# Layer 3's first batch projected inside layer 2's last batch, and projections led by four steps

## The reference, cut to what matters

```python
# layer 2: masked attention with 8 heads of 16
scores = einsum('bhnd,bhmd->bhnm', q, k) / sqrt(D)
w = softmax(where(mask, -inf, scores), axis=-1)
out = einsum('bhnm,bhmd->bhnd', w, v)          # then @ Wo.T + bo
# layer 3: graph attention with 8 heads of 16
Wh = (h @ W).reshape(b, n, H, HD).transpose(0, 2, 1, 3)
e = e1[:, :, :, None] + e2[:, :, None, :]      # e1 = Wh @ a1, e2 = Wh @ a2
e = where(mask, -inf, e); e = where(e >= 0, e, 0.2 * e)
h_prime = einsum('bhij,bhjd->bhid', softmax(e, axis=-1), Wh)
```

## Time and profile before

| | us |
|---|---|
| runs | 745.53, 745.69, 747.58 (median 745.69) |
| profiled execution, time | 745.24 |
| its span, first to last instruction | 743.5 |
| TensorE busy | 663.1 (89%) |
| VectorE busy | 604.3 (81%) |
| ScalarE busy | 541.3 (73%) |
| GpSimd busy | 493.5 (66%) |
| mean granted TensorE clock | 0.972 |

### The profile page before, as it was taken

One profiled execution on the slowest core, in us unless ns is written; L12 is line 12 of the kernel. 1 busy time (PEld: TensorE's weight loads), 2 busy tenths in 40 slices (PEclk: granted clock), 3 DMA queues, 4 the chain that ended last, 5 costly groups with the idle time before them and its releaser, 6 DMA issues.

```text
span 743.5 us, 17518 instructions
## 1 busy us (share of the span) xinstructions
PE 663.1 (89%) x6402; PEld 495.5 (67%) x6402; DVE 604.3 (81%) x1534; ACT 541.3 (73%) x855; POOL 493.5 (66%) x522
## 2 busy tenths in 40 slices
PE   2999699999679999999999996899999999999973
PEld 1788577777446766666666666677777777777752
DVE  3599859999677888888888884888888888888882
ACT  1555389988468777777777773598888888888882
POOL 6377529999765466656667654466766677777685
PEclk9999999999789999999999998999999999999996
DMA  8900000000000000000000000000000000000001
GB/s 233 282 4 1 1 1 1 2 1 2 0 1 2 1 2 3 1 2 1 2 2 2 2 2 0 2 2 2 29 17 16 15 16 16 17 28 16 16 16 42
DMA packets 28885, 14.91 MB, mean 20 GB/s; under 512 B 1920, under 2 KB 28800, under 8 KB 28800
## 3 DMA queue, kind: packets, MB, share of 16 engines
q1 hardware_dynamic: 25344, 12.59, 6.1%
q10 hardware_dynamic: 3456, 1.20, 0.8%
HBM read 9.59 MB, written 4.19 MB: 19 GB/s over the span
## 4 chain that ended last, share of the span: by engine, by line
PE 59%; DVE 12%; issue 11%; POOL 9%; ACT 5%; POOLq 4%; DVEq 0%; ACTq 0%
PE pair L1009 20%; POOL X L528 5%; PE pair L1140 5%; PE quad L1107 4%; POOLq L523 4%; PE pair L1201 4%; DVE arena L987 2%; DVE nmx L993 2%; PE quad L1057 2%; PE pair L1112 2%; PE pair L1126 2%; PE pair L1118 2%; PE pair L1076 2%; PE quad L1047 2%; PE quad L1068 2%
## 5 line engine op out<-in xcount | busy, mean ns | idle before, releaser
L630 POOL TENSOR_TENSOR arena<-arena,nmx 128x1024 f32<-128x1024 f32 x64 | 121.3, 1895 | 90.5 <-DVE nmx L933 88.9
L644 POOL TENSOR_TENSOR arena<-arena,nmx 128x1024 f32<-128x1024 f32 x64 | 121.3, 1896 | 82.7 <-DVE nmx L993 82.7
L1009 PE MATMUL pair<-identf,arena 128*128 128x128 f32 x1088 | 152.0, 282 | 0.5 <-ACT arena L831 0.5
L1009 PEld LDWEIGHTS pair<-identf,arena 128*128 128x128 f32 x1088 | 117.9, 142 | 31.0 <-issue 30.3
L528 POOL TENSOR_SCALAR X<-yb,ln 128x128 f32<-128x128 f32 x256 | 113.5, 455 | 9.0 <-issue 9.0
L522 POOL TENSOR_TENSOR ln<-ln,neghalf 128x4 f32<-128x4 f32 x64 | 66.6, 1041 | 37.9 <-DVE ln L562 37.8
L818 ACT ACTIVATE arena<-quad 128x1024 f32<-128x1024 f32 x64 | 66.1, 1033 | 31.5 <-PE quad L1191 31.5
L926 DVE TENSOR_TENSOR arena<-quad,mask 128x1024 f32<-128x1024 f32 x64 | 77.7, 1215 | 4.8 <-PE quad L1107 4.1
L933 DVE TENSOR_REDUCE nmx<-arena 128x8 f32<-128x1024 f32 x64 | 78.0, 1218 | 1.7
L993 DVE TENSOR_REDUCE nmx<-arena 128x8 f32<-128x1024 f32 x64 | 78.0, 1218 | 1.7
L987 DVE TENSOR_TENSOR arena<-quad,arena 128x1024 f32<-128x1024 f32 x64 | 77.7, 1214 | 0.0
(11 more groups left out here) (203 smaller groups left out, 1438.4 us busy)
## 6 DMA issues: line engine op xcount, KB each, us to landing
X<-in_x SPq DMA_DIRECT2D x16, 256.0 KB, 5.8
arena<-in_adj SPq DMA_DIRECT2D x16, 256.0 KB, 6.3
out<-X SPq DMA_DIRECT2D x16, 256.0 KB, 2.3
nat_all<-in_L_gnn_W ACTq DMA_DIRECT2D x2, 64.0 KB, 4.8
w<-in_L_gnn_W ACTq DMA_DIRECT2D x2, 64.0 KB, 5.5
nat_all<-in_L_gnn_W_loop ACTq DMA_DIRECT2D x1, 64.0 KB, 2.6
nat_all<-in_L_gnn_Wg_loop ACTq DMA_DIRECT2D x1, 64.0 KB, 3.2
hg_bias<-in_L_gnn_b_loop ACTq DMA_DIRECT2D x1, 64.0 KB, 5.1
```

The source lines that it names most:

```text
L630: nc.gpsimd.tensor_tensor(v3(P2[t % 3], HEADS), v3(P2[t % 3], HEADS), nmx2[t % 2][:].unsqueeze(2).broadcast_to([128, HEADS, N]), ALU.add)\
L644: nc.gpsimd.tensor_tensor(v3(p, HEADS), v3(p, HEADS), nmx2[(t - 1) % 2][:].unsqueeze(2).broadcast_to([128, HEADS, N]), ALU.add)\
L1009: last = nc.tensor.transpose(dst[:, cols(i)], src[:, cols(i)], identf[:])
```

## The change

Layer 3's step t now goes with layer 2's step 64 + t, five steps sooner. The first batch of layer 3 is prepared within layer 2's steps 60 to 64 (new branches of `layer2`: X transposes in bank 6, the other three pieces in bank 7). Scores of graphs 0 to 5 are issued at the head of `layer2`'s step in TensorE's list (`LAP = 6`). `AHEAD` is 4 in place of 5, so from batch 1 on every piece comes one step later against the scores (X transposes at j=0, logit terms j=1, terms' transposes j=2, values j=3; the split at j=2), and ScalarE's copy of the values now stands behind its pT copy, ahead of the scaling, one step later. Layer 3's buffers in turn are shifted (`rows_of`, `y_of`, `out_bank`, `pv_bank`), with waits for layer 2's last readers. New functions `scores`, `logit_terms`, `terms_back`, `values` and `split_e` hold the same instructions as before; removed lines that only moved into them are cut, and so are the renamings of `P2[...]` to `rows_of(...)` on GpSimd and ScalarE.

```diff
@@ -46 @@
-AHEAD, BEHIND = 5, 13
+AHEAD, BEHIND = 4, 13
+LAP = 6
@@ -82 @@
         layer2(t)
-    for t in range(-AHEAD, GRAPHS + BEHIND):
-        layer2(GRAPHS + AHEAD + t)
+    for t in range(GRAPHS + BEHIND):
+        layer2(GRAPHS + t)
         layer3(t)
@@ -222 @@
         def y_of(L, b):
-            return yb[b % 4 if L == 3 else b % 2]
+            return yb[(b + 2) % 4 if L == 3 else b % 2]
@@ -233 @@
-        def early(t):
-            return bank[3] if t < 0 else bank[6]
+        def rows_of(t):
+            return P2[(t + GRAPHS) % 3]
+        def pv_bank(g):
+            return bank[6] if g < GRAPHS - 1 else bank[4]
...
         def out_bank(b):
-            return bank[6] if b < BATCHES - 2 else bank[4]
+            return bank[5] if b == BATCHES - 2 else bank[6]
@@ -537 @@
             if L == 3:
-                if b < 2:
-                    dve.wait_ge(sem("L2_norm_done"), BATCHES - 1 + b)
+                if b in (2, 3):
+                    dve.wait_ge(sem("L2_norm_done"), BATCHES - 3 + b)
                 need(dve, sem("L3_norm_done"), b - 3)
@@ -762 @@
                     nc.scalar.copy(xT[(b + 1) % 2][:], proj(t - 1)).then_inc(sem("L2_xT"), 1)
+                if t in (GRAPHS - 3, GRAPHS + 1):
+                    first = t - GRAPHS + 3 >> 2
+                    act.wait_ge(sem("L3_xT_mm"), first + 1)
+                    nc.scalar.copy(xT[first][:], bank[6]).then_inc(sem("L3_xT"), 1)
+                if t == GRAPHS - 1:
+                    act.wait_ge(sem("L3_eT_mm"), 1)
+                    nc.scalar.copy(eT[0][:], bank[7].bitcast(BF16)[:, 0:W]).then_inc(sem("L3_eT"), 1)
+                if t == GRAPHS:
+                    act.wait_ge(sem("L3_v_mm"), 1)
+                    act.wait_ge(sem("L2_pv_mm"), GRAPHS - G)
+                    nc.scalar.copy(vx[0][:].rearrange("p (a c) -> p a c", c=HP)[:, :, 0:HD],
+                                   v3(bank[7], G * HEADS)).then_inc(sem("L3_v"), 1)
                 if j == 1 and real(b):
@@ -786 @@
                     need(act, sem("L2_out_mm"), t - 4)
-                    nc.scalar.copy(oT[(t - 3) % 2][:], bank[6][:, 0:2 * N]).then_inc(sem("L2_oT"), 1)
+                    nc.scalar.copy(oT[(t - 3) % 2][:], pv_bank(t - 3)[:, 0:2 * N]).then_inc(sem("L2_oT"), 1)
                 if graph(t - 1):
@@ -803 @@
                 b, k = (t + AHEAD - 1) // G, (t + AHEAD - 1) % G
-                if real(b):
-                    if k == 0:
+                if real(b) and b > 0:
+                    if k == 0 and b > 1:
                         act.wait_ge(sem("L3_xT_mm"), b + 1)
                         need(act, sem("L3_v_mm"), b - 1)
-                        nc.scalar.copy(xT[b % 2][:], early(t - 1)).then_inc(sem("L3_xT"), 1)
+                        nc.scalar.copy(xT[b % 2][:], bank[6]).then_inc(sem("L3_xT"), 1)
                     if k == 2:
...
                         need(act, sem("L3_s_mm"), G * (b - 1))
-                        nc.scalar.copy(eT[b % 2][:], early(t - 1).bitcast(BF16)[:, 0:W]).then_inc(sem("L3_eT"), 1)
+                        nc.scalar.copy(eT[b % 2][:], bank[6].bitcast(BF16)[:, 0:W]).then_inc(sem("L3_eT"), 1)
+                    if k == 3:
+                        act.wait_ge(sem("L3_v_mm"), b + 1)
+                        need(act, sem("L3_pv_mm"), G * (b - 1))
+                        nc.scalar.copy(vx[b % 2][:].rearrange("p (a c) -> p a c", c=HP)[:, :, 0:HD],
+                                       v3(bank[6], G * HEADS)).then_inc(sem("L3_v"), 1)
                 if graph(t):
@@ -820 @@
                     nc.scalar.copy(oT[g % 2][:], bank[7][:, 0:2 * N]).then_inc(sem("L3_oT"), 1)
-                if k == 3 and real(b):
-                    act.wait_ge(sem("L3_v_mm"), b + 1)
-                    need(act, sem("L3_pv_mm"), G * (b - 1))
-                    nc.scalar.copy(vx[b % 2][:].rearrange("p (a c) -> p a c", c=HP)[:, :, 0:HD],
-                                   v3(early(t - 1), G * HEADS)).then_inc(sem("L3_v"), 1)
...
+        def split_e(dve, b, o):
+            e = v3(o[:, 0:G * 2 * HEADS], G)
+            dve.wait_ge(sem("L3_e_mm"), b + 1)
+            need(dve, sem("L3_eT_mm"), b)
+            for part in range(3):
+                at = v3(ep[:], G)[:, :, 32 * part:32 * part + 2 * HEADS]
+                need(dve, sem("L3_split"), 5 * b + 2 * part)
+                nc.vector.tensor_copy(at, e).then_inc(sem("L3_split"), 1)
+                if part < 2:
+                    dve.wait_ge(sem("L3_split"), 5 * b + 2 * part + 1)
+                    nc.vector.tensor_tensor(e, e, at, ALU.subtract).then_inc(sem("L3_split"), 1)
@@ -925 @@
                       .then_inc(sem("L2_masked"), 1)
+                if t == GRAPHS - 2:
+                    split_e(dve, 0, bank[7])
                 if j == 2 and real(b - 3):
@@ -968 @@
                 b, k = (t + AHEAD - 1) // G, (t + AHEAD - 1) % G
-                if k == 1 and real(b):
...
+                if k == 1 and real(b) and b > 0:
+                    split_e(dve, b, bank[6])
                 b, j = t // G, t % G
                 if graph(t - 1):
-                    p = P2[(t - 1) % 3]
+                    p = rows_of(t - 1)
+                    if t <= 3:
+                        dve.wait_ge(sem("L2_pT_mm"), GRAPHS - 3 + t)
+                    if t <= 2:
+                        dve.wait_ge(sem("L2_less_max"), GRAPHS - 2 + t)
                     dve.wait_ge(sem("L3_scaled"), t)
@@ -1076 @@
+            def scores(t):
+                b, j = t // G, t % G
+                if not graph(t):
+                    return
+                if j == 0:
+                    pe.wait_ge(sem("L3_eT"), b + 1)
+                if t < 2:
+                    pe.wait_ge(sem("L2_masked"), GRAPHS)
+                need(pe, sem("L3_leaky"), t - 1)
+                for i in range(2):
+                    o = bank[2 * (t % 2) + i]
+                    mm(o, identb[:], heads_of(mask2, b, j), start=True, stop=False)
+                    mm(o, eT[b % 2][:, cols(j)], sel1[:, cols(i, HQ * 128)], start=False, stop=False)
+                    for h in range(HQ):
+                        last = mm(o[:, cols(h)], sel2[:, cols(HQ * i + h)], eT[b % 2][:, cols(j)],
+                                  start=False, stop=h == HQ - 1)
+                last.then_inc(sem("L3_s_mm"), 1)
+            def logit_terms(b, o):
+                for i in range(G):
+                    last = mm(o[:, cols(i, 2 * HEADS)], xT[b % 2][:, cols(i)], wh_w[:, D:], start=True, stop=True)
+                last.then_inc(sem("L3_e_mm"), 1)
+            def terms_back(b, o):
+                pe.wait_ge(sem("L3_split"), 5 * (b + 1))
+                for i in range(G):
+                    last = nc.tensor.transpose(o.bitcast(BF16)[:, cols(i)], ep[:, cols(i)], identb[:])
+                last.then_inc(sem("L3_eT_mm"), 1)
+            def values(b, o):
+                for i in range(G):
+                    last = mm(o[:, cols(i)], xT[b % 2][:, cols(i)], wh_w[:, 0:D], start=True, stop=True)
+                last.then_inc(sem("L3_v_mm"), 1)
             def back(b):
...
                     need(pe, sem("L2_oT"), G * (b + 2))
+                elif b == BATCHES - 2:
+                    pe.wait_ge(sem("L2_pT"), GRAPHS)
                 else:
-                    pe.wait_ge(sem("L2_pT"), GRAPHS)
-                    need(pe, sem("L2_y_done"), b)
+                    pe.wait_ge(sem("L3_v"), 2)
                 pe.wait_ge(sem("L2_on"), G * (b + 1))
@@ -1106 @@
                     last.then_inc(sem("L2_s_mm"), 1)
+                if GRAPHS <= t < GRAPHS + LAP:
+                    scores(t - GRAPHS)
+                if t == GRAPHS - 2:
+                    pe.wait_ge(sem("L3_xT"), 1)
+                    pe.wait_ge(sem("L2_v"), BATCHES)
+                    pe.wait_ge(sem("L2_on"), t - 4)
+                    logit_terms(0, bank[7])
+                if t == GRAPHS:
+                    pe.wait_ge(sem("L3_eT"), 1)
+                    pe.wait_ge(sem("L2_on"), t - 4)
+                    values(0, bank[7])
                 if j == 1 and real(b):
@@ -1124 @@
                     mm(first_q(b), qT_w[:], xT[1 - s][:], start=True, stop=True).then_inc(sem("L2_q_mm"), 1)
+                if t == GRAPHS - 1:
+                    pe.wait_ge(sem("L2_on"), t - 4)
+                    terms_back(0, bank[7])
                 g = t - 3
@@ -1132 @@
                         pe.wait_ge(sem("L2_xT"), b + 2)
+                    if t == GRAPHS - 3:
+                        pe.wait_ge(sem("L3_xT"), 1)
+                    if t == GRAPHS + 1:
+                        pe.wait_ge(sem("L3_xT"), 2)
                     if j == 3:
...
                     for h in range(HEADS):
-                        last = mm(bank[6][HP * (h % 4):HP * (h % 4) + HP, cols(h // 4)],
+                        last = mm(pv_bank(g)[HP * (h % 4):HP * (h % 4) + HP, cols(h // 4)],
                                   vx[g // G % 2][:, cols(HEADS * (g % G) + h, HP)], pT2[g % 2][:, cols(h)],
```

(98 more changed lines are left out.)

2 lines of the change are left out of this document (1 added, 1 removed).

## The result

| | us |
|---|---|
| kernel before, median of the runs beside it | 746.63 |
| changed kernel, four runs | 737.48, 739.13, 739.21, 739.22 (median 739.17) |
| ratio, with 95% interval | 0.989 (0.9867 to 0.9913) |
| profiled execution of the changed kernel, time and span | 739.22 and 737.5 |

The change is faster by 1.1%. The medians differ by 7.5 us, the profiled executions by 6.0 (745.24 and 739.22); 740.8 was forecast, counted from the profiled execution.

What follows compares the result with a forecast made beforehand. TensorE carries most of the chain of waits, but no one busy share decides, so each stage was read by its order. 5.1 - 2.0 - 2.9 - 1.6 + 5.85 = 4.45 us less than 745.24 gave 740.8; range 734 to 746.

Steps and rivals of the forecast that it cites:

- Last batch of layer 2 and the walk: Seam, order followed: layer 3 starts 18.6 us earlier, graph 8's scores only 5.1 us earlier; bounds 3.5 and 8.5.
- S3(0): Start of the scores of layer 3's graph 0, put at 450.35 in place of 468.97.
- S3(2): Start of the scores of layer 3's graph 2, put at 461.65 after waiting for leaky(0).
- S3(8): Start of the scores of layer 3's graph 8, put at 492.1 in the walk; 497.15 before.
- S3(3): Start of the scores of layer 3's graph 3, put at 467.85, with 1.2 us added by the low clock.
- The port: Steps 66 and 70: two VectorE statistics operations held beside GpSimd's subtraction, 0.7 and 1.3 us, together -2.0.
- The clock: Seam: TensorE's clock falls to the low level for 6.8 us, -2.9; bounds 0 and 3.4.
- Left over from layer 2: Steps 72 to 75: layer 2's last statistics and normalisation fall into layer 3's steps, -1.6; bounds 0 and 3.
- Steady state: Layer 3's batches: X transposes stop waiting for the values copy, 0.45 us a batch, +5.85 over 13; bounds 0.55 and -0.3.
- y's loop: Steady batch, from ON of j=2 round through GpSimd's y: 15.4 us and a few handovers; period taken as 15.58.
- Tail: Work after the scores of graph 60: no projections in either kernel, so 0.
- Rival (c): Steady batch: y becomes the bound and the kernel slower, 751 us at a period of 16.4; chance 0.08.

Runs made afterwards that it cites:

- e8: Changed kernel with layer 2's last aggregates after leaky, 15 unread matmuls at the seam, second stats pair later and two GpSimd scalings behind y: 727.64 us.
- e4: Changed kernel with 15 unread 128x512 bf16 matmuls put into TensorE's gaps of step 66: 738.42 us.
- e1: Kernel before with a lead of 4 and ScalarE's values copy ahead of the scaling, without the overlap at the seam: 740.58 us.
- e2: Changed kernel with ScalarE's values copy put back behind oT for batches 2 to 15, lead still 4: 745.06 us.
- e5: Changed kernel with layer 3's second pair of batch statistics moved from the end of VectorE's step j=2 to step j=3: 742.12 us.
- e7: Changed kernel with both the second stats pair later on VectorE and the first two GpSimd scalings moved behind y: 734.65 us.
- e11: Changed kernel run once more beside the others, with no edit: 739.00 us.
- e6: Changed kernel with layer 3's first two scalings of a batch moved on GpSimd from j=3 to behind y at j=0: 734.69 us.
- e10: Changed kernel with layer 2's last aggregates after leaky, second stats pair later and y sooner, without unread matmuls: 729.67 us.

## Why the prediction was right

Direction and range were right, and so were the mechanisms: 740.8 forecast, 739.2 measured, the forecast itself and not a rival. That the number came so close is in part luck. Of the 8.1 us from step 60 on, 4.45 had been forecast; 2.1 lost ahead of step 60, of which the text said nothing, hid more than half of that error. The forecast put 0.2 on the stretch to graph 8, 4.25 on the steady part with what is left over, and 0 on the tail; measured are 1.6, 5.4 and 1.1, each of them more. By its steps:

- *Last batch of layer 2 and the walk.* S3(0) was put at 450.35; less the 2.09 of offset it came at 450.57. S3(2): 461.65 forecast, 461.45 measured; the waits of 1.1, 1.6 and 2.9 are the rows 0.85, 1.35 and 2.68. For S3(8) without the held operations and the clock, 492.1 was forecast; e8, which has neither, gives 435.23 + 56.3 = 491.5. From S3(3) to S3(8) the starts of the forecast's walk are 0.5 to 1.0 us later than those of e8. The queue order was the mechanism: 18.4 us at the start of the layer, 1.6 at graph 8. (One entry of TensorE's sum, 0.46 for X's transposes, is 0.43 by its own rows, 0.68 less 0.25; nothing hangs on it.)
- *The port.* Both operations were held, 1.46 and 1.45 us, at the steps named, and the first ends at 466.74, where GpSimd's subtraction does (466.72). The second ends at 490.36, GpSimd's at 490.33. Forecast 0.7 and 1.3 on the path, measured 0.7 and 1.2 up to graph 7's scores, and 1.5 at graph 8's in place of 2.0. Moved away from the subtraction, the operation takes 0.17. With that the trace agrees with the rule of the Trainium skill ("SBUF — State Buffer", "SBUF: two separate sides") for the large subtraction; beside GpSimd's 4-column power operation (512.33 to 513.35) the same operation took 0.17 at 512.90, and was not held.
- *The clock.* It fell, at 469, for 6.8 us, as forecast. The price was put at 2.9; e4 gives 2.5 for this execution, and 1.1 where the stretch was 3.4 long. The term was somewhat too large, and took for given a length that varies. It was also placed too early: 1.2 was put on S3(3), which comes 32.9 us after step 60 in the changed kernel and in e4 alike, and the whole 2.5 comes between S3(3) and S3(4). TensorE's gaps ahead of the fall were 0.85, 1.35 and 2.68 us. (Of the two gaps that the prediction names for the kernel before, the clock fell at 460.1, 0.7 us into the one of 1.97.) The Trainium skill's advice ("TensorE: Matmul & The Clock Gate", "Why this matters for your kernels") would have had the clock stay up; here it did not, and short matmuls in two of those gaps, 5 and 10 of them, kept it up.
- *Left over from layer 2.* Batches 8 to 12 and 12 to 16 take 16.34 and 16.37, together 1.75 above two steady ones; forecast 1.6. e1, without the overlap, has nothing of it (15.42 and 15.51 against 15.49). A third statistics operation was held there, 0.67 us at 505.66, until GpSimd's subtraction ended.
- *Steady state.* Mechanism right, and shown by e1 and e2; size 0.55 a batch where 0.45 was taken, which is the bound that the text gave. The allowance for handovers in y's loop was not needed: the changed kernel's batch is 15.48, and PV's loop and y's are within 0.06 us of each other, as e5 to e7 show. PV's wait stayed at 0.5 and VectorE's wait for y came to 0.65, as expected there.
- *Tail.* Forecast 0; 1.1 less in the profile, with the clock falling 9.0 us from the end in place of 13.7. e11, the same kernel with 15.7, has 0.3 more than before. So nothing of the 1.1 can be put down to the change.

Rival (c), y as the bound, named the right place: y's loop is the longer of the two that set the new period, but at 15.48 and not at 16.4.

## What to carry to other kernels

When a step is moved earlier on several in-order queues, write down for each queue what then stands ahead of the next layer's work: here 18 us at the start of the layer shrank to under 2, while moving one 0.6 us copy ahead of a waiting instruction gave 0.5 us in each of 13 batches. Where a period has two waits of about the same size on different engines, removing one hardly moves the period (0.0 and 0.06 us here, 0.4 together); test them together before calling either harmless. And compare profiles from a landmark just ahead of the change, as spans carry microseconds from places that the change doesn't touch.

## What the runs showed of the hardware

A stretch at 1.2 GHz at the seam lasted 6.8 us in one execution of a kernel and 3.4 in another, and cost 2.5 and 1.1 us, against e4; in four kernels (e1, e5, e6, e10) a second one of 3.4 us followed, 10.2 us after the first had ended in e1 and 3.4 in the others. Six or ten unread 128x512 bf16 matmuls in a gap of 2.7 us, with five in one before it, kept TensorE at 2.4 GHz in all three kernels that had them. A 4-column VectorE operation of 0.17 us that came while GpSimd's subtraction of 128x1024 ran ended only with it: the four times that this happened in the changed kernel it took 0.69, 1.46, 1.45 and 0.67 us, and 1.99 once in the kernel before.
